# Finer setup loads and rewritten orders of all engines in a fused two-layer decoder kernel

## The chip, the cores and the metric

The kernel runs on one core of a Trainium2 chip. The metric is the device time of one execution in microseconds (us): the median of three runs. An engine is one of TensorE (PE in the profile, with its weight loads as PEld), VectorE (DVE), ScalarE (ACT), GpSimd (POOL) and SyncE (SP), which only issues DMA transfers here.

## What is computed

Input x has 32 sequences of 128 rows and 256 columns in float32. Six sublayers follow each other, each added to x and then normalised over its 256 columns:

```python
x = _layernorm(x + _L0_attn_ref(x, ...))                # 16 heads, a window of 7 keys, softmax times a learnt one
x = _layernorm(x + _L0_xattn_ref(x, ctx_1024, ...))     # cross attention, masked
x = _layernorm(x + _L0_ffn_ref(x, L0_ffn_Wr, ...))      # 8 experts pick 16 of 128 rows each, rope, attention, scatter back
x = _layernorm(x + _L1_attn_ref(x, ...))                # attention with a decay mask
x = _layernorm(x + _L1_xattn_ref(x, ctx_1024, ...))     # one context row chosen by argmax, then 16 heads
x = _layernorm(x + _L1_ffn_ref(x, ...))                 # quantised 256 -> 1024 -> 256 with a convolution and silu
```

The window attention is the part that the change touches most:

```python
scores = jnp.einsum('bhld,bhlwd->bhlw', Q, Kw) / np.float32(np.sqrt(DH))
fw = attn * conn
fw = fw / (fw.sum(axis=-1, keepdims=True) + 1e-09)
out = jnp.einsum('bhlw,bhlwd->bhld', fw, Vw)            # Kw, Vw: keys and values shifted by -3 to 3 rows
```

## The kernel before

The 32 sequences are worked on in 16 groups of two (256 rows). Each group passes nine stations, which the code names by a letter: Q (queries, keys and values of the window attention), A (the rest of the window attention), B (cross attention), X (experts), C (attention with decay), D (the choice of a context row), E (the 16 heads on it), F (the quantised feed-forward), and once, for the whole kernel, S (the setup: constants loaded, products of weights formed, the two feed-forward weights rounded). On every engine a station is a generator that stops at each `yield`; one stretch between two `yield`s is a step. A string of letters for each engine, `ORDER` (lines 68 to 121), says which station takes its next step, and `walk` plays it:

```python
for name in order:
    if name not in live or next(live[name], done) is done:
        live[name] = stations[name](next(left[name]))
        next(live[name])
```

So the tables fix the order of instructions on each engine, and semaphores alone fix the times: an engine that meets a wait stands there, and everything behind it in its table with it. Several groups are under way at once, each at another station. Banks of PSUM are tied to stations: Q and A share `bank_a`; B, C and D share `bank_c`; X has `bank_x`, F `bank_f`, E the four `banks_e`. Before a step writes a bank, `take` waits until the step that reads the last content is done, mostly a ScalarE copy (line 1377).

What the prediction speaks of, with its lines:
- SP's queue (lines 366 to 446) issues all transfers. In `setup`, S steps load weights: `wqkv_e` (3 MB) and `wo_e` (1 MB), the experts' weights, stand in the fourth loop over names (line 401). In `queries`, the second step waits for `a_v`, the copied values, and issues the twelve shifts (line 426): transfers inside SBUF that lay the values of a group one to three rows higher or lower. The next group's input `xT0` is loaded right behind (line 377).
- TensorE: Q's three steps project queries, keys and values (`wq0`, `wk0`, `wv0`, all by line 456). A's steps form head sums (line 562), turn the scores (line 570), turn the summed values (line 579, after `a_summed`) and project them with `wo0`. The next group's `wv0` has to wait for that projection's sum (`a_added`). B's first two steps are `w_cross` and `wv0x`.
- VectorE: A's window sum is thirteen steps (lines 1101 and 1105, `SUM_STEPS`), behind waits for all twelve shifts (`shift_in`) and the softmax weights. The same engine adds each sublayer's result to x (line 918) and forms, in the setup, the decay mask (lines 993 to 1006) and the column sums of the second feed-forward weight (line 1039).
- ScalarE rounds the two feed-forward weights in pieces (lines 1433, 1442, 1446); `small` is the sum of magnitudes that their scale needs, and `bank_f <- small` is the TensorE step that adds it over rows.

## Time and profile before

| | |
|---|---|
| median of 3 runs | 1081.63 us (1080.34 to 1083.15) |
| the profiled execution's own time | 1083.18 us |
| its span in the profile | 1081.4 us |
| instructions | 20184 |
| TensorE busy | 938.1 us, 87% |
| VectorE busy | 864.5 us, 80% |
| ScalarE busy | 774.6 us, 72% |
| GpSimd busy | 165.1 us, 15% |
| mean granted TensorE clock | 0.957 of 2.4 GHz |

All rows are of one profiled execution. Times count from the start of its span; the execution takes 1.8 us more than the span. A row in order of time reads: start, duration, engine, line, operation, what is written and what is read, count of merged instructions, and in brackets how long the engine was idle before and what released it.

### The profile page before, as it was taken

To read this page: it belongs to the slowest core of one execution; us is meant where nothing else is said; L and a number is where in the kernel's file an instruction comes from. 1 tells how busy PE (TensorE), PEld (TensorE's weight loads), DVE (VectorE), ACT (ScalarE), POOL (GpSimd) and SP (SyncE) were. 2 spreads that over 40 slices of the span, in tenths; PEclk is the share of its full clock that TensorE was granted. 3 is DMA by queue.
4 is the path that set the end of the run, shared out by engine and by line. 5 is a ranking of instruction groups with operands and counts; after the bars stand their busy time and mean duration, and the time that the engine had idled before them with its cause. 6 is when DMAs were issued, how large, how long until landed. Compare 5 with 4: busy or idle time off the path is not lost.

```text
span 1081.4 us, 20184 instructions
## 1 busy us (share of the span) xinstructions
PE 938.1 (87%) x7318; PEld 685.2 (63%) x7318; DVE 864.5 (80%) x2281; ACT 774.6 (72%) x1921; POOL 165.1 (15%) x404
## 2 busy tenths in 40 slices
PE   6588798999998999999999999999999888887652
PEld 4455566767776676767676777777676666565321
DVE  5585775789888979898899989898989785866754
ACT  2166564768877878877788878787878787867653
POOL 2010210202103030302021211212020201010000
PEclk9789999999999999999999999999999999998765
DMA  9723112030120203030302011121102000000000
...
DMA packets 36626, 59.04 MB, mean 55 GB/s; under 512 B 6656, under 2 KB 15872, under 8 KB 36016
## 3 DMA queue, kind: packets, MB, share of 16 engines
...
## 4 chain that ended last, share of the span: by engine, by line
PE 55%; ACT 18%; DVE 17%; issue 3%; SPq 2%; DMA 2%; POOL 1%; ACTq 0%; POOLq 0%; DVEq 0%
PE bank_c L456 15%; PE bank_a L456 8%; PE banks_e L456 6%; PE bank_x L456 6%; PE bank_f L456 4%; PE bank_x L666 3%; ACT squares_out L1389 2%; SPq L426 2%; ACT area_e L1605 2%; DVE area_f L1314 2%; DVE neg_top L1254 2%; PE banks_e L835 2%; DMA area_a<-in_xT 2%; ACT area_f L1652 2%; PE bank_a L562 2%
## 5 line engine op out<-in xcount | busy, mean ns | idle before, releaser
L1314 DVE SCALAR_TENSOR_TENSOR area_f<-area_f,w_convw 128x254 f32<-128x254 f32 x256 | 111.7, 478 | 9.2 <-ACT area_f L1639 7.5
L1254 DVE TENSOR_REDUCE neg_top<-banks_e 128x8 f32<-128x1024 f32 x64 | 76.2, 1220 | 30.1 <-PE banks_e L456 29.9
L1377 ACT ACTIVATE area_bx<-bank_x 128x512 f32<-128x512 f32 (+1 forms) x144 | 70.1, 499 | 27.7 <-PE bank_x L666 11.5
L1101 DVE TENSOR_TENSOR area_a<-area_a 128x512 f32<-128x512 f32 x112 | 74.7, 683 | 10.9 <-DMA area_a<-area_a 10.3
L1639 ACT ACTIVATE area_f<-area_f,w_convb,w_convw 128x256 f32<-128x256 f32 x128 | 69.8, 596 | 15.0 <-DVE area_f L1305 14.8
L1046 DVE TENSOR_TENSOR area_a<-area_a 128x512 f32<-128x512 f32 x112 | 73.4, 683 | 5.1 <-PE bank_a L562 2.9
L1605 ACT ACTIVATE area_e<-banks_e 128x512 f32<-128x512 f32 x128 | 68.3, 601 | 8.9 <-PE banks_e L835 8.7
L1377 ACT ACTIVATE area_bx<-bank_c 128x512 f32<-128x512 f32 x64 | 34.3, 536 | 52.9 <-PE bank_c L456 39.4
L1105 DVE TENSOR_TENSOR area_a<-area_a 128x512 f32<-128x512 f32 x96 | 65.8, 685 | 0.3
L1377 ACT ACTIVATE area_a<-bank_a 128x512 f32<-128x512 f32 (+1 forms) x80 | 43.9, 549 | 30.8 <-PE bank_a L456 21.2
L456 PE MATMUL bank_x<-area_bx 128*128 128x128 f32 (+1 forms) x256 | 51.9, 336 | 5.8 <-ACT area_bx L1377 4.3
L456 PE MATMUL bank_a<-area_a,w_wq 128*128 128x256 f32 x128 | 37.1, 442 | 19.1 <-DMA area_a<-in_xT 19.1
L456 PEld LDWEIGHTS bank_x<-area_bx 128*128 128x128 f32 x256 | 40.8, 191 | 17.5 <-ACT area_bx L1377 8.5
L1305 DVE TENSOR_TENSOR area_f<-bank_f,area_f 128x512 f32<-128x512 f32 x64 | 43.8, 684 | 7.7 <-PE bank_f L456 7.7
L456 PE MATMUL bank_f<-area_f,w1q 128*128 128x256 bf16 x256 | 41.8, 290 | 9.3 <-DVE area_f L1305 7.9
L1644 ACT ACTIVATE area_f<-area_f 128x512 f32<-128x512 f32 x64 | 40.4, 632 | 13.0 <-DVE area_f L1314 12.6
L1678 POOL TENSOR_SCALAR bn_negmean_b<-bn_sums_b 128x2 f32<-128x2 f32 x16 | 4.7, 294 | 288.8 <-DVE x L918 288.8
L666 PE MATMUL bank_x<-w_wqkv_e,area_bx 128*32 128x384 f32 x512 | 47.9, 492 | 0.0
L1377 ACT ACTIVATE area_e<-banks_e 128x256 bf16<-128x256 f32 (+1 forms) x64 | 34.5, 540 | 15.6 <-PE banks_e L821 6.8
L1324 DVE SCALAR_TENSOR_TENSOR area_f<-area_f 128x512 f32<-128x512 f32 x64 | 43.8, 684 | 2.1 <-ACT area_f L1644 1.5
L456 PE MATMUL banks_e<-chosen_key,chosen_q 32*128 32x256 f32 x512 | 38.6, 417 | 7.0 <-DVE neg_top L1254 3.9
L1652 ACT ACTIVATE area_f<-area_f 128x512 f16<-128x512 f32 x64 | 37.6, 624 | 9.4 <-DVE area_f L1362 9.4
...
## 6 DMA issues: line engine op xcount, KB each, us to landing
...
```

The costliest lines, as they stand in the source:

```text
L456: last = pe.matmul(out_ap, l, r, start=i == 0 and not opened, stop=closes and i == len(pairs) - 1)
L666: last = pe.matmul(bank_x[ES * q:ES * (q + 1), 0:3 * HP], xgf[:, c, e, :], wq[:, c, e, :], start=c == 0, stop=c == DC - 1)
L1046: return dve.tensor_tensor(product_of(wi).rearrange("p (n t) -> p n t", t=P), qT0.rearrange("p c (b t) -> p (c b) t", t=P), kT0.rearrange( ...
L1101: made[wi] = own.mark(dve.tensor_tensor(v4, v4, bc(e4[:, :, wi, :], 3, DH), ALU.mult))
L1105: added = dve.tensor_tensor(vw[:, to, :], vw[:, to, :], vw[:, wi, :], ALU.add)
L1254: dve.tensor_reduce(top[:, b, r:r + 2, :, 0].rearrange("p r (par c) -> p r c par", c=DC), banks_e[:, r:r + 2, :].rearrange("p r (c par k) ...
L1305: dve.tensor_tensor(blocks(th_f[jj % 3], 2), blocks(bank_f[:, :], 2), bc(tscale_f, 1, 2), ALU.mult).then_inc(f_h, 1)
L1314: last = dve.scalar_tensor_tensor(c4[:, i, :, dst], h4[:, i, :, src], cwt3[:, 2 * jj + i, k:k + 1], c4[:, i, :, dst], ALU.mult, ALU.add)
L1377: return act.activation(dst, src, ACT.Copy)
L1605: act.activation(pT_e[:, r * 4 * P:(r + 1) * 4 * P], bank_e[r][:, :], ACT.Exp, scale=float(DH) ** -0.5).then_inc(e_exp, 1)
L1639: last = act.activation(c4[:, i], h4[:, i], ACT.Identity, bias=w["convb"][:, j:j + 1], scale=cwt3[:, j, 1:2])
L1652: act.activation(n2_f[jj], c_f[jj], ACT.Copy, bias=ROUND16).then_inc(f_round, 1)
```

## The change

The setup's loads on SP are cut into smaller steps: 14 in place of 9. The six arrays of the connectivity network are a step apart from the other early constants, each of `wq0`, `wk0`, `wv0` is a step, and `wqkv_e` and `wo_e` are a step each. The first projection waits for `wq0` and the first input only; the wait for `wk0` and `wv0` stands ahead of the second. The tables of all five engines are new. No compute instruction is changed, added or left out. The diff, of whose tables one line each is shown:

```diff
 ORDER = {
     "PE": (
-        "QQQASSAASSSQBQBAADQSABBAASBBQBQXXBAAXSQXXABXBAAXBXQBXXBXXQXABAXCXQAXBXBXBABXACQXCXQCXXXCAXCAXBXQAXDDXDX"
+        "QQQASSSSSABABSQQDSAAQABABABBBSQXQXBAXAXQXABXABAXXBBXXQXBXQXBAXAXCQCXAXBAXABXBBQXCQXCXXCXCXAXAXBQDXADDXAX"
...
     "SP": (
-        "SQSBSASSSQQSSADSBQQQQBAAQQBADQQDBAQQBBQDQFAQQDFADBQQFBAFQQADBDQQFBAFAQBQDFBQAQDBQQFADFQDQABDFBAQDDFDFFFF"
+        "SSSQSSSSBASSSSQQSSDSABAAAAQQBQQBQQQDQBQQDBDQBQFAFDAQQBDFQAQBFDAQQBDFAQQBDFAQQBDFABQQDFABQQQFDAQBDFAQBDFD"
...
@@
             def setup(_):
-                for name in ("wq0", "wk0", "wv0"):
-                    sp.dma_start(w[name][:, :], io[name]).then_inc(qkv_in, 16)
-                yield
+                for name, sem in (("wq0", xt_in), ("wk0", kv_in), ("wv0", kv_in)):
+                    sp.dma_start(w[name][:, :], io[name]).then_inc(sem, 16)
+                    yield
                 for dst, name in ((c1, "c1"), (b1, "b1"), (c2, "c2"), (b2, "b2"), (c3, "c3"), (b3, "b3")):
                     sp.dma_start(dst, io[name]).then_inc(early2_in, 16)
+                yield
                 for name in ("pos", "ident", "headsum", "rows", "part", "wo0"):
                     sp.dma_start(w[name][:, :], io[name]).then_inc(early_in, 16)
                 yield
@@
-                for name in ("cos_sin", "blk", "iota128", "wqkv_e", "wo_e"):
+                for name in ("cos_sin", "blk", "iota128"):
                     sp.dma_start(w[name][:, :], io[name]).then_inc(xw_in, 16)
                 yield
+                for name in ("wqkv_e", "wo_e"):
+                    sp.dma_start(w[name][:, :], io[name]).then_inc(xw_in, 16)
+                    yield
@@
             def queries(g):
-                pe.wait_ge(xt_in, 16 * (g + 1))
+                pe.wait_ge(xt_in, 16 * (g + 2))
                 if g:
                     pe.wait_ge(a_heads, 2 * g)
-                if g == 0:
-                    pe.wait_ge(qkv_in, 16 * 3)
                 take("a")
                 project(bank_a, chunked("wq0"), xT0).then_inc(a_qk_proj, 1)
                 until("a", a_qk, 2 * g + 1)
                 yield
+                if g == 0:
+                    pe.wait_ge(kv_in, 16 * 2)
                 take("a")
```

Where the new tables put things is told by the instructions in their order, here at three places. **SP's queue around the first group's shifts**, before:

```order
L401 DMA w_iota<-in_iota 128x128
L401 DMA w_wqkv_e<-in_wqkv_e 128x6144
L401 DMA w_wo_e<-in_wo_e 128x2048
L426 DMA area_a<-area_a 112x512
L426 DMA area_a<-area_a 13x512
```

and now:

```order
L402 DMA w_iota<-in_iota 128x128
L405 DMA w_wqkv_e<-in_wqkv_e 128x6144
L405 DMA w_wo_e<-in_wo_e 128x2048
L430 DMA area_a<-area_a 112x512
L430 DMA area_a<-area_a 13x512
```

The experts' weights stand ahead of the first group's shifts (the 112-row and 13-row pieces of `area_a`) in both.

**TensorE from the last product of weights to group 0's window values**, before (`bank_e` holds products of weights; the `wq`, `wk` rows are group 1's, `w_cross`, `wv0x`, `headsum` group 0's):

```order
L456 MATMUL banks_e<-area_s,onesb 32x256
L456 MATMUL bank_a<-area_a,w_wq 128x256 [waits a_shifted,a_heads,xt_in]
L456 MATMUL bank_a<-area_a,w_wq 128x256 x3
L456 MATMUL bank_c<-area_bx,w_cross 128x256 [waits ctx_b_in,cross_in,setup_dve,setup_act]
L456 MATMUL bank_c<-area_bx,w_cross 128x256 x3
L456 MATMUL bank_a<-area_a,w_wk 128x256 [waits a_qk]
L456 MATMUL bank_a<-area_a,w_wk 128x256 x3
L466 MATMUL bank_c<-bias_parts,ones_bf 128x512 [waits b_kav]
L456 MATMUL bank_c<-w_wv0x,area_bx 128x256 x4
L579 MATMUL bank_a<-w_ident,area_a 128x128 [waits a_qk,a_summed]
```

and now:

```order
L460 MATMUL banks_e<-area_s,onesb 32x256
L566 MATMUL bank_a<-area_a,w_headsum 32x256 [waits a_prod]
L566 MATMUL bank_a<-area_a,w_headsum 32x256 x5
L460 MATMUL bank_c<-area_bx,w_cross 128x256 [waits ctx_b_in,cross_in,setup_dve,setup_act]
L460 MATMUL bank_c<-area_bx,w_cross 128x256 x3
L574 MATMUL bank_a<-w_ident,area_a 128x112 [waits a_scores]
L574 MATMUL bank_a<-w_ident,area_a 128x112
L470 MATMUL bank_c<-bias_parts,ones_bf 128x512 [waits b_kav]
L460 MATMUL bank_c<-w_wv0x,area_bx 128x256 x4
...
L460 MATMUL bank_a<-area_a,w_wq 128x256 [waits a_shifted,a_heads,xt_in]
...
L460 MATMUL bank_f<-small,onesb 128x1 [waits setup_act]
L583 MATMUL bank_a<-w_ident,area_a 128x128 [waits a_qk,a_summed]
```

Group 0's two projections of cross attention (`w_cross`, `wv0x`) stood behind group 1's first projection, which waits for `xt_in`; now they stand ahead of it. The line numbers are four higher in the changed kernel. The step on `small`, which waits for ScalarE's pass over the first feed-forward weight, now stands ahead of the turned values (`a_summed`).

**VectorE at group 2's window sum**, before (L1101 and L1105 are the sum's steps, `x_spread` belongs to group 0's experts):

```order
L1105 TENSOR_TENSOR area_a<-area_a 128x512 [waits dve_own]
L1204 RECIPROCAL area_bx<-area_bx 128x2 [waits x_exp]
L1101 TENSOR_TENSOR area_a<-area_a 128x512
L1105 TENSOR_TENSOR area_a<-area_a 128x512 [waits dve_own]
L1039 TENSOR_REDUCE area_s<-w2q 128x256 [waits setup_act]
L1101 TENSOR_TENSOR area_a<-area_a 128x512
L1105 TENSOR_TENSOR area_a<-area_a 128x512 [waits dve_own] x2
L1046 TENSOR_TENSOR area_a<-area_a 128x512 [waits a_qk]
L1046 TENSOR_TENSOR area_a<-area_a 128x512
L918 SCALAR_TENSOR_TENSOR x,bn_sums_x<-bank_x,x 128x256 [waits x_spread]
```

and now, first at two of group 2's key products and then at the end of the sum (line numbers are four higher):

```order
L1050 TENSOR_TENSOR area_a<-area_a 128x512
L1043 TENSOR_REDUCE area_s<-w2q 128x256 [waits setup_act]
L1050 TENSOR_TENSOR area_a<-area_a 128x512 [waits a_heads]
L1050 TENSOR_TENSOR area_a<-area_a 128x512
...
L1105 TENSOR_TENSOR area_a<-area_a 128x512
L1109 TENSOR_TENSOR area_a<-area_a 128x512 [waits dve_own]
L1105 TENSOR_TENSOR area_a<-area_a 128x512
L1109 TENSOR_TENSOR area_a<-area_a 128x512 [waits dve_own]
L1105 TENSOR_TENSOR area_a<-area_a 128x512
L1109 TENSOR_TENSOR area_a<-area_a 128x512 [waits dve_own] x2
L922 SCALAR_TENSOR_TENSOR x,bn_sums_x<-bank_x,x 128x256 [waits x_spread]
```

The reduction of `w2q` stood among the thirteen steps of the sum. It now stands between key products of the same group, behind a wait for ScalarE's finished rounding, and the sum ends without it.

## Rows read from the trace of the kernel before

**Rows 1.** The page's parts 1 and 2: busy time, the span in 40 slices.
```profile
PE 938.1 (87%) x7318; PEld 685.2 (63%) x7318; DVE 864.5 (80%) x2281; ACT 774.6 (72%) x1921; POOL 165.1 (15%) x404
...
PE   6588798999998999999999999999999888887652
```

**Rows 2.** Stretches: length; busy PE, PEld, DVE, ACT, POOL; clock, DMA share, GB/s.
```profile
60.00:120.00 60.00, 45.52 (x280) 32.61 (x273) 47.28 (x115) 37.16 (x83) 6.91 (x12) 0.90 0.25 74
...
200.00:840.00 640.00, 610.29 (x5006) 452.76 (x5004) 570.06 (x1516) 514.39 (x1301) 110.98 (x261) 1.00 0.17 50
...
960.00:1080.00 120.00, 67.10 (x458) 42.36 (x456) 75.37 (x172) 69.74 (x150) 8.33 (x24) 0.75 0.02 8
```

**Rows 3.** Issues on SP's queue, 16 to 28 us.
```profile
16.82 0.43 SPq L401 DMA_DIRECT2D w_wqkv_e<-in_wqkv_e  x1
...
18.50 8.73 SPq L426 DMA_DIRECT2D area_a<-area_a  x12
27.28 0.53 SPq L377 DMA_DIRECT2D area_a<-in_xT  x1
```

**Rows 4.** VectorE in order of time, 39 to 80 us.
```profile
39.72 1.89 DVE L1101 TENSOR_TENSOR area_a<-area_a 128x512 f32<-128x512 f32 x3 [10.32 <-DMA area_a<-area_a]
...
71.55 1.90 DVE L1101 TENSOR_TENSOR area_a<-area_a 128x512 f32<-128x512 f32 x3
...
78.19 1.41 DVE L1105 TENSOR_TENSOR area_a<-area_a 128x512 f32<-128x512 f32 x2
```

**Rows 5.** TensorE in order of time, 40 to 58 us.
```profile
40.19 3.78 PE L456 MATMUL bank_a<-area_a,w_wq 128*128 128x256 f32 x8 [9.62 <-DMA area_a<-in_xT]
43.76 3.13 PE L456 MATMUL bank_c<-area_bx,w_cross 128*128 128x256 f32 x8
48.56 1.99 PE L456 MATMUL bank_a<-area_a,w_wk 128*128 128x256 f32 x8 [1.67 <-ACT area_a L1377]
...
50.61 1.89 PE L456 MATMUL bank_c<-w_wv0x,area_bx 128*128 128x256 f32 x8
52.34 0.60 PE L579 MATMUL bank_a<-w_ident,area_a 128*128 128x128 f32 x4
...
56.78 1.97 PE L456 MATMUL bank_a<-w_wv,area_a 128*128 128x256 f32 x8
```

**Rows 6.** VectorE in order of time, 105 to 119 us.
```profile
105.75 0.48 DVE L918 SCALAR_TENSOR_TENSOR x<-bank_c,area_bx,x 128x256 f32<-128x256 f32 x1 [3.63 <-PE bank_c L456]
...
106.60 1.89 DVE L1101 TENSOR_TENSOR area_a<-area_a 128x512 f32<-128x512 f32 x3
...
112.69 3.64 DVE L1039 TENSOR_REDUCE area_s<-w2q 128x256 f32<-128x2048 f16 x1
...
116.85 1.40 DVE L1105 TENSOR_TENSOR area_a<-area_a 128x512 f32<-128x512 f32 x2
```

**Rows 7.** TensorE in order of time, 101 to 122 us.
```profile
101.33 3.44 PE L456 MATMUL bank_a<-area_a,w_wq 128*128 128x256 f32 x8 [1.99 <-DMA area_a<-in_xT]
104.61 1.03 PE L456 MATMUL bank_c<-area_bx 128*128 128x256 f32 x4
...
112.75 1.89 PE L456 MATMUL bank_x<-area_bx 128*128 128x256 f32 x8
118.31 1.12 PE L579 MATMUL bank_a<-w_ident,area_a 128*128 128x128 f32 x4 [3.67 <-DVE area_a L1105]
...
119.64 2.74 PE L456 MATMUL bank_c<-w_wv0x,area_bx 128*128 128x256 f32 x8
```

**Rows 8.** ScalarE in order of time: two pieces of the second weight's rounding.
```profile
82.90 1.91 ACT L1433 ACTIVATE w2q<-area_f 128x2048 f16<-128x2048 f32 x1
...
101.63 0.71 ACT L1446 ACTIVATE w2q<-area_f,small 128x512 f16<-128x512 f32 x1
```

**Rows 9.** TensorE's longest waits between 200 and 840 us: total, times, longest.
```profile
PE bank_c L456 <- ACT area_d L1377: 6.5, 14, 0.7
PE banks_e L456 <- ACT area_e L1377: 2.4, 5, 0.7
```

More of the change, by code:

```diff
@@ L97 @@
-        "FCFFFFEEFFFFFFFEEFFFDFDDFFFEFEEFFFEEEEEEFFFFFFFFEEFFFFFFFFFFFEEFFFFFFFEFFFFFFFFFFFFFFFFFFFFFFFFFFFFFFF"
+        "SSSSQQQQASSSSASASSSSSSSSSSSSSSSSSSSSSSSSSAASAAAAASSSSSSSSSSSAAAAAAAAAAAAASSSQQQQAASSSSSSAASSSBBAABAAAAAB"
+        "AAAAAAASAAAAAASXXXXXXXXXQXQQAAXQSAASXXXBBAAXXAAAAABBXAAAAAAAAAAAAAXQQQQAXXXAXXXXXXXXAAAABBAAXBAXXBAAAAAA"
+        "AAAXXACCXAAAAACQQQQCXAAXXXXXXAXXXADXXDDAAAAAAAAAAAAXXXAAAEEBBEXEEEEEBAXQBAAQXQQAAEECCCXEECEAAXXXXXXFFFXX"
+        "XDDDAAXXFEEFEFFEFEEEEFFBBFBFXXXFBFAFAFXFXAFAAFFAAFAAFCCEAEACXAAAAACAAAAFFFXFEEFQQQFFQEDDDXXXXXXAFFFFAXXX"
@@ new lines @@
+        "AXEEXAEEEEFEEFFFFBBFFBFFFFBXXXFFAAFFFEEAXAXAFXAAFACFCAAAFFCFAAAACEFEAFFFXQQQAAAEAQFXXXXXXXXFFFXAAXXDDDFA"
+        "EEFFEEFEEFEEFBBFFBXAFXBXFFFFAXAXFFAAAFEEXFFAAFAACCAACAAAAAACFFFAAEAXFEFQFFQQQEFAAXDDDFFFXXXXXXXXAEEXXAEE"
+        "FEEEEFFFFBBFFBFFFBFXFXFXAAFFFEFXEXFAAAXAAFAAACACAAAAAEECFFFXFFCFFAAQQQEFAAQFFFDXDDXXXXXAAXXFXFEFEFFEXEXF"
+        "FEEAEEFBBAFFXBXXFFBFFAAFFFXEXEAAAFXAAFAACCAAAAAFFFCAAEEFFFFCAXAAAFQQEQQXXXXXXXXDDDXAAFFFXXEEFEEFFFFEEFEB"
+        "EBFABAFFXXFBFXFFFAAFFFEAAXXFEAAAFCCAACAAAAAAAXAFFFCAXEEAAFFFFQQQQEFDDDFAXXXFFXXXAXXXEEXXFEEFFFEEFEAFEFBB"
@@ new lines @@
+        "FAFFBFXBXFFXFAAFFAAXXFFAAAXAAFCCFFAACEEFAAAAACXAFFEEAFFQQQQAAEDDDXXXXXFXFFFXXXAAEEXXEFEFFFFEEEBBFEFBFFAA"
+        "FFXXBXFFFFFAAEFFEAXXFAACAXFFCFAACAAAAACAEAAAEAAAXFFFFQQQEDDDQFXXXFFFXXXEEAAEEXEEFXEXEXFFFBFBFFBFXAAFFFXX"
+        "FXBFAFAFXEXEFFXAAAAAAAFAAFAAAACCFFCFAQAACEAEXAFQQFFFQEAAXXXXXXXXXFFFFXXAADDDFFEEFFEEFEEBEFBEFFBXXFFFFXBF"
+        "AAFFFFAFEXEXAFAAAXAACCAACAAAECAAAAFFXAEFAFFQQQQFFEXDXDDXXXFXXXAAFFFXEXEXFEEFEFFEEEFBFBFFBAFAFFXXFXFBFAFA"
+        "EFAEAAAAAAFFXXFCCXFFFAACAAEFEFCFFXAAAAAEAAFXDXXDDXXFAFFXXXXEEXXFEEFFFEEEEFBFBFFBFXXXFBFFFXXEEFFXFFFFCCFF"
@@ new lines @@
+        "XCXXACXCAXBXQDXADAXDAXBXDDDQBXBCBQEXEEEEXBECXBXCEEEEXECCXECADXCEXDXAEDAQFFDFDDDXFBBFFBXAFFEBXBFFEEEEXFCA"
+        "EFFCBQFXCFXBXCQCXEEEEXCEDCXDFFEXDXAFFEXEADFQDDDAFFFBFBXFBXFEFFBEEFFBEEFXFECAFXABCFQFXCEFBXEEXECQECXXCDFF"
+        "FEXFCXXEXBADEFDFFFAQDFXDDDFABBFXFFXEBFBFFEEEEXAFCEFABCFXFBFXCEEEEXCECXQXCQDCXDEAFFDFFXEXFEXAFQDFDDDFAFBB"
+        "XFBEXFFFBEEFBFEEAFXECFFBCFXFBAXCFXEEXEEQXECXQCXEFCFFFXCDEDXFEDFXAFFDFADDDFAQBFFFBXBFXEFBXEEBEEAFFFCXEAFB"
+        "CXFBFCXQXEEEDEXCEXCFFQFFCXECXXDEXFDAFEDADDDFFAQFBFBXBFFXFBFEXBFFEEEECAFEFFCAXFQBXCFXBXCQXEEEECXECXDCEFDF"
@@ new lines @@
+        "AFFXDEXEFDXADDDFFFQAFBFBXFBFFXFEBFBXFEEFEEAFCEXFABCFXBQCFXXCXDXCEEEECEXCQDFEXDFFFXEXEDAFDDDFAFFBFAFBFBQX"
+        "FFBXFFBEFXFEEEEACFFECFAXBCFXBXEEEECXQECXCXQCDDEXFDFFFXXEDAXEDDDFFFFBAFBAFQBXFFFBXBFFEXFEEEEFAFEXCFABXCQX"
+        "FBCFXQXEEEECXCECDXEACXXFFEFFXBEQDAFDAFFFXDFADDDFXBFFBXFBEFFCFBEEEEFXFAEFBFCFBXCEEEXECXECXQXCDCXDQEXXDFFF"
+        "XFEAEDFDDDFFFAFQBAFBXBFFFBXFFEFXEEBEEAFFECFABFXCBEECFXEXEXCEXCXFFECFFDCXDEXXDAXEFDFDDDFFAFBAFBXBFFFXBEFF"
+        "XBFEEEEXBECFFXCXFFBCXFEEEEXCEXFCFFFXECDXXCEDXFEDFFFFDDDDXFXCFCFFXCFFFECFCEEEFXFECFEFCDXDEEXEEFDXFEXFFXEX"
@@ L112 @@
+        "DEXDDDEFCFCFFCFEFCEFCFEEEFCDFEFFCEFFEEEDFFEFDEFFDFFDDDEFEFFFFEFEEEEFFFEFFFEFFFEEEFFEEFFFFEFEFFFFFFFFFFFF"
         "FFFFFFFFFF"
@@ L114 @@
     "POOL": (
[L115 removed]
+        "ABABXABCXABXCEABCXEAFBCXEFABCXEFABXCEFABCXFEABCXEFABCXEFABCXEFABCXEAFBCXEFABCXEFABXCEFCXEFCEFEFF"
     ),
     "SP": (
[L118 to L119 removed]
+        "SSSQSSSSBASSSSQQSSDSABAAAAQQBQQBQQQDQBQQDBDQBQFAFDAQQBDFQAQBFDAQQBDFAQQBDFAQQBDFABQQDFABQQQFDAQBDFAQBDFD"
+        "FDFFFF"
     ),
```

51 lines of the change are left out of this document (12 added, 39 removed).

## The prediction

> **What bounds the kernel now.** The page's busy shares come first: TensorE is busy 87% of the span, VectorE 80% [rows 1]. The 40 slices say where the rest is: TensorE's digits are 5 to 8 in the first five slices, 8 or 9 in nearly all of the middle, and fall over the last six [rows 1]. So there are three regimes, and the table of stretches gives their size [rows 2]. Between 200 and 840 us TensorE works 610.3 of 640 us: 29.7 us, 5%, are left. In the last 120 us it works 67.1, and the granted clock is 0.75 there: the last groups go through F alone, each step waiting for the one before. Between 60 and 120 us it works 45.5 of 60 us: too few groups are under way.
>
> The order of time shows what holds the beginning. SP issues the experts' weights at 16.8 us and the first group's shifts from 18.50 to 27.23 us [rows 3]. VectorE starts the window sum at 39.72 us after 10.3 us of idleness that a transfer ends [rows 4], and TensorE starts group 1's query projection at 40.19 us after 9.6 us, ended by the input that was issued at 27.28 us [rows 3, 5]. From there the window attention is a chain over groups: values of group g copied, twelve shifts issued (8.7 us), window sum, values turned and projected with `wo0`, sum added to x, values of group g+1 projected. What shortens this chain early starts everything else earlier, as every transfer that sets a fixed time lies before 50 us.
>
> **The wait at 39.7 us stays.** The finer setup steps would allow the experts' 4 MB to be issued after the shifts. The instructions in order say that they are not: `wqkv_e` and `wo_e` stand directly ahead of the shifts as before. The shifts then queue behind the same bytes, and I cost the loads' part at nothing. The two waits on `wk0`/`wv0` and on `xT0` gain nothing either: the input is issued last of the four, and the first projection waits for it. The table's new place of the first x and context loads is covered by the same wait.
>
> **Start, group 0 and 1: -3.2 us.** TensorE now does group 0's `w_cross` and `wv0x` in the idle stretch before 40 us; before, they lay between group 1's query projection and group 0's value turning (3.13 and 1.89 us at 43.76 and 50.61 [rows 5]). VectorE's decay products, which lay among the thirteen sum steps, move there too. So after 39.72 the sum takes 8.05 us (thirteen steps undisturbed: from 71.55 to 79.60 [rows 4]) and ends at 47.8. TensorE: query projection 40.19 to 44.0 (3.78), a copy of some 0.6, key projection 2 to 3 us, another copy: 48.3. The step on `small` waits for the first feed-forward weight, which ScalarE reads by about 47.5. I let the value turning start at 48.9. From it to the next value projection it is 4.44 us now (52.34 to 56.78 [rows 5]): 53.4 against 56.78, so 3.4 less, of which I take 3.2. The cover that has to hold is VectorE's: softmax of group 0 and the decay mask must end before 39.7. By the durations of the same instructions they end at about 39.2; if not, up to 1 us is lost.
>
> The clock: the query projection at 40.19 took 3.78 us and the key projection at 48.56 took 1.99 for the same eight matmuls [rows 5]; TensorE had been idle 9.6 us before the first. I assume 3.78 again, since an idle stretch of only 1.99 us also had 3.44 behind it at 101.33 [rows 7]. The Trainium skill (TensorE: Matmul & The Clock Gate, What's actually happening) says that activity releases the throttle; by it the two projections moved into the gap could keep the array at 2.4 GHz and give 1.8 us more. That is not in the sum.
>
> **Group 2: -4.8 us more.** Before, VectorE's sum of group 2 was held twice. First by its place behind group 1's cross attention result, idle 3.63 us to 105.75 [rows 6]: TensorE had group 3's query projection ahead of that product, which waited for its input and ran 3.44 us [rows 7]. In the new table the product stands ahead of the query projection. Second by the reduction of `w2q` among the steps, 3.64 us at 112.69 [rows 6]; now it is done earlier, in front of two key products, where VectorE has gaps. With the 3.2 us from before, the sum could end 10.5 us earlier than its 118.25, at 107.8. TensorE waited 3.67 us for it at 118.31 [rows 7]. Now TensorE is the later one: from 101.33 to the end of the experts' product at 112.75 + 1.89 = 114.64 it had 13.3 us, less 1.4 for what went ahead and 1.5 at full clock, plus 2 for `wv0x` of group 2, now in front of the turning (2.74 at the lower clock, at 119.64 [rows 7]). Starting with the input at 98.1, the turning comes at about 110.5 instead of 118.3. I take 8.0 us for the beginning in all. Bounds: 3.2 if nothing of group 2 comes, 10.5 if all of it does.
>
> **Middle: -4.5 us.** The macro order is the same: 97% of TensorE's 952 steps stand within five places of where they stood. So what is won at the beginning moves the middle as a whole; it isn't lost in it. What changes is how often two steps of one station follow each other directly, so that the second waits for the copy of the first: on TensorE 75 pairs before and 42 now, in the middle (142nd to 810th step) 25 and 5. What such a pair costs is in the waits: 14 of D's cost 6.5 us, 5 of E's 2.4 us [rows 9], about 0.47 us each. Twenty pairs fewer are 9.4 us of the 29.7 at most. The waits are ended by ScalarE and VectorE, and VectorE works 570 of the 640 us [rows 2]: TensorE, coming earlier, will meet some of them at the next step. I take half, 4.5 us (bounds 0 and 9.4; below 0 is the slower rival's case). The Trainium skill (Trace Analysis, Matmuls) wants independent groups to rotate through PSUM banks so that a copy overlaps the next group's matmuls; here pairs on one bank fall from 78 to 46, and by that rule all 9.4 would come.
>
> **End: -1.0 us.** In the last 142 steps pairs fall from 28 to 22, worth at most 2.8 us, but the last 19 steps are the same and wait for each other. I take 1.
>
> **SP's queue** is passed in another order too: the store of group 1 and the load of x for group 7 now stand ahead of group 7's shifts. Group 1's result was ready 9 us before those shifts were issued, so this costs nothing; x of groups 2 to 5 is loaded at once near 40 us, 1 MB that nobody waits for.
>
> **The sum.** 8.0 + 4.5 + 1.0 = 13.5 us. The profiled execution took 1083.2 us, which makes 1069.7; the median of the runs is 1.6 us lower, so the forecast is **1068 us**.
>
> **Rivals.**
> - *Only the start comes* (0.20): TensorE is so full after 125 us, and its waits so much those of other engines, that the middle gives nothing and group 2 little: 3.2 us, 1078.4 us. For it: 5% idle in the middle is close to full. Against it: the 3.67 us at 118.31 are plainly TensorE's and go.
> - *All waits go* (0.10), as the rule on banks has it: 10.5 + 9.4 + 2.8 = 22.7 us, 1059 us. Against it: VectorE at 89% in the middle.
> - *The rounding becomes the bound, slower* (0.08): VectorE's reduction of `w2q` waits for ScalarE's last piece. Before, ScalarE began the second weight at 82.90 and ended at 102.34 [rows 8], without anybody waiting. Now group 2's key products, head sums and softmax are queued behind it on VectorE. If ScalarE ends only at 99 (3.2 earlier), the reduction ends at 102.7, the sum starts 8 us later, at about 110.5 instead of 106.6, and the kernel takes 4 us more: 1085.6 us. The new table puts all eight pieces ahead of the experts' gathered rows, so by it they should be done at about 83. It decides from 95 us on. Other slower orders, a bank held in the middle, get 0.01.
> - *The change does more than the order tells* (0.01): if the shifts landed before the experts' weights, the sum would start 10 us earlier: 1058 us.
>
> The forecast itself has 0.60. About 0.3% (3.2 us) is what a measurement can tell from no change: 1078.4 to 1084.8 is "same". Half of the first rival lies there, the rest of it is faster. Faster 0.80, same 0.11, slower 0.09. The range from 1059 to 1079 us holds the forecast with all its bounds, the first rival and about half of the second.
>
> **What would show it.** In the changed profile the first sum step starts at 39.7 us still; group 1's value projection at about 53.5; group 2's value turning at 110 to 111; the reduction of `w2q` lies between 84 and 90 us; the stretch from 200 to 840 has 612 to 616 us of TensorE work; waits of `bank_c` for `area_d` fall from 14 to about 4; the last 120 us look the same. I am wrong if the value turning of group 2 comes after 115, or if the middle's idle time is 30 us or more.

## The result, and the profile after

| | before | changed |
|---|---|---|
| median | 1082.39 us (1080.34 to 1085.33, 4 runs) | **1053.27 us** (1051.58 to 1054.91, 4 runs) |
| ratio | | 0.973, 95% interval 0.970 to 0.976 |
| profiled execution / its span | 1083.18 / 1081.4 us | 1052.96 / 1051.2 us |

It is 29 us faster, where 13.5 were forecast, and lies 6 us below the range of 1059 to 1079 us. The page of the changed kernel, parts 1 and 2, against [rows 1]:

```profile
PE 932.7 (89%) x7318; PEld 681.6 (65%) x7318; DVE 868.3 (83%) x2281; ACT 774.7 (74%) x1921; POOL 159.9 (15%) x404
...
PE   6779989999999999999999999999899999876642
```

The work is the same 7318 matmul records, and they take 5.4 us less of busy time, in part because fewer of them run at the lower clock (below, at group 2); the fifth slice (105 to 131 us) went from 7 to 9, and there are three digits of 8 where there were nine. Once one kernel is ahead, the same moment finds the two at different work. But 97% of TensorE's steps stand within five places of where they stood, so the number of matmul records that are done is a ruler that both share ("equal progress" from here on). First the kernel before, cut at 120, 240 and 840 us, then the changed one, cut where it had done as many (columns as in [rows 2]):

```profile
0.00:120.00 120.00, 83.35 (x450) 60.57 (x451) 80.09 (x202) 50.17 (x111) 14.40 (x36) 0.89 0.51 166
120.00:240.00 120.00, 109.98 (x849) 80.74 (x851) 81.97 (x228) 73.33 (x195) 16.66 (x44) 0.99 0.20 62
240.00:840.00 600.00, 573.42 (x4721) 424.97 (x4713) 540.83 (x1434) 486.31 (x1229) 105.52 (x245) 1.00 0.16 49
840.00:1082.00 242.00, 171.33 (x1311) 118.88 (x1307) 161.62 (x419) 164.78 (x388) 28.53 (x79) 0.86 0.04 11
```

```profile
0.00:107.00 107.00, 81.85 (x450) 59.26 (x451) 81.18 (x203) 50.58 (x111) 15.02 (x37) 0.90 0.58 191
107.00:222.20 115.20, 108.80 (x844) 79.46 (x846) 82.57 (x225) 73.31 (x191) 16.87 (x44) 1.00 0.19 60
222.20:815.30 593.10, 573.27 (x4729) 425.08 (x4722) 542.69 (x1435) 486.10 (x1231) 100.77 (x244) 1.00 0.16 49
815.30:1052.00 236.70, 168.81 (x1307) 117.80 (x1305) 161.85 (x421) 164.69 (x391) 27.30 (x80) 0.87 0.03 11
```

So 13.0 us are won by the old 120 us, 4.8 from there to 240, 6.9 in the middle (TensorE's idle time there: 26.6 us before, 19.8 now) and 5.5 at the end (counted to the ends of the spans, 1081.4 and 1051.2). The forecast had 8.0 for the first two together, 4.5 and 1.0.

**The start.** SP's queue, VectorE and TensorE of the changed kernel in order of time, against [rows 3 to 5]:

```profile
18.06 8.73 SPq L430 DMA_DIRECT2D area_a<-area_a  x12
```

```profile
38.66 1.90 DVE L1105 TENSOR_TENSOR area_a<-area_a 128x512 f32<-128x512 f32 x3 [0.68 <-DMA area_a<-area_a]
```

```profile
32.06 1.89 PE L460 MATMUL bank_c<-w_wv0x,area_bx 128*128 128x256 f32 x8
...
39.13 3.78 PE L460 MATMUL bank_a<-area_a,w_wq 128*128 128x256 f32 x8 [0.49 <-DMA area_a<-in_xT]
43.59 3.78 PE L460 MATMUL bank_a<-area_a,w_wk 128*128 128x256 f32 x8 [0.69 <-ACT area_a L1381]
...
48.42 0.64 PE L583 MATMUL bank_a<-w_ident,area_a 128*128 128x128 f32 x4
...
52.90 1.96 PE L460 MATMUL bank_a<-w_wv,area_a 128*128 128x256 f32 x8 [0.96 <-DVE x L922]
```

The transfer still ends the wait ahead of the sum. That it comes 1.06 us earlier is no more than scatter: in the profiles below with SP's old order the sum starts at 39.1 to 40.7 us, in those with the new one at 38.6 to 40.0 (run 13, the same kernel again: 39.99). Of VectorE's 10.32 us of idleness there 0.68 are left, as setup work fills them. Group 1's value projection comes at 52.90 (forecast 53.5, before 56.78).

**Group 2**, against [rows 6, 7]:

```profile
84.26 3.81 DVE L1043 TENSOR_REDUCE area_s<-w2q 128x256 f32<-128x2048 f16 x1
...
97.58 1.87 DVE L1105 TENSOR_TENSOR area_a<-area_a 128x512 f32<-128x512 f32 x3
...
104.19 1.41 DVE L1109 TENSOR_TENSOR area_a<-area_a 128x512 f32<-128x512 f32 x2
```

```profile
97.22 1.99 PE L460 MATMUL bank_a<-area_a,w_wq 128*128 128x256 f32 x8
...
107.81 0.60 PE L583 MATMUL bank_a<-w_ident,area_a 128*128 128x128 f32 x4
...
112.80 1.89 PE L460 MATMUL bank_a<-w_wv,area_a 128*128 128x256 f32 x8
```

The values are turned at 107.81 instead of 118.31, and nothing is waited for there; group 3's value projection follows at 112.80, where before it came at 126.02: 13.2 us earlier. TensorE, before, between the rows of [rows 7]:

```profile
105.47 0.38 PE L492 MATMUL bank_x<-w_ident,area_bx 128*128 128x128 f32 x2
106.33 0.71 PE L456 MATMUL bank_x<-area_bx 128*128 128x128 f32 x4 [0.47 <-ACT area_bx L1377]
...
109.92 1.07 PE L456 MATMUL bank_x<-w_wo_e,area_bx 128*32 128x256 f32 x16 [0.69 <-ACT area_bx L1377]
```

The clock is part of it. Before, it was granted at 0.66 on average from 100 to 105 and from 117 to 122 us (query projection 3.44 us, `wv0x` 2.74 [rows 7]); in the changed kernel it is whole there, and the two take 1.99 and 1.89 us:

```profile
72.00:952.00 880.00, 833.80 (x6792) 615.70 (x6790) 758.93 (x2016) 694.23 (x1756) 143.26 (x356) 1.00 0.15 45
```

**The middle.** TensorE's longest waits, 200 to 840 us, against [rows 9]:

```profile
PE bank_c L460 <- ACT area_d L1381: 2.7, 6, 0.8
PE banks_e L460 <- ACT area_e L1609: 2.2, 6, 0.6
```

The two kinds of waits that I had priced (for the copies into `area_d` and `area_e`) had 6.5 + 2.4 us; the first has 2.7 now, in 6 waits, and the second is no longer in the list. The row of `area_e` shown is another wait of E, for ScalarE's exponentials (line 1609); before it had 0.6 us.

### The profile page after: what moved, and what is told of

It reads as the page before. It is cut to its first block, busy times and chain, and to the rows that moved or that the text cites. A ratio compares the mean times of both kernels' runs of the same rounds, so it can differ in the third digit from the quotient of the medians.

```text
span 1051.2 us, 20184 instructions
## 1 busy us (share of the span) xinstructions
PE 932.7 (89%) x7318; PEld 681.6 (65%) x7318; DVE 868.3 (83%) x2281; ACT 774.7 (74%) x1921; POOL 159.9 (15%) x404
## 4 chain that ended last, share of the span: by engine, by line
PE 58%; ACT 18%; DVE 16%; issue 3%; SPq 2%; POOL 2%; DMA 1%; ACTq 0%; POOLq 0%; DVEq 0%
PE bank_c L460 16%; PE bank_a L460 8%; PE banks_e L460 6%; PE bank_x L460 6%; PE bank_f L460 4%; DVE neg_top L1258 3%; DVE area_f L1318 3%; ACT area_e L1609 3%; PE bank_x L670 3%; ACT squares_out L1393 2%; PE banks_e L839 2%; PE bank_a L566 2%; ACT area_f L1643 2%; ACT area_f L1656 2%; DVE x L922 2%
## 5 line engine op out<-in xcount | busy, mean ns | idle before, releaser
L1258 DVE TENSOR_REDUCE neg_top<-banks_e 128x8 f32<-128x1024 f32 x64 | 76.0, 1221 | 17.9 <-PE banks_e L460 17.5
L1381 ACT ACTIVATE area_bx<-bank_x 128x512 f32<-128x512 f32 (+1 forms) x144 | 70.4, 500 | 25.2 <-PE bank_x L670 11.5
L1105 DVE TENSOR_TENSOR area_a<-area_a 128x512 f32<-128x512 f32 x112 | 74.7, 683 | 1.3 <-DMA area_a<-area_a 0.7
L1309 DVE TENSOR_TENSOR area_f<-bank_f,area_f 128x512 f32<-128x512 f32 x64 | 43.7, 683 | 12.7 <-PE bank_f L460 12.5
L1648 ACT ACTIVATE area_f<-area_f 128x512 f32<-128x512 f32 x64 | 40.7, 636 | 13.0 <-DVE area_f L1318 12.8
L460 PE MATMUL banks_e<-area_e,chosen_v 128*32 128x512 f32 x256 | 35.0, 620 | 11.9 <-ACT area_e L1609 11.6
L1366 DVE TENSOR_TENSOR area_f<-area_f,bank_f 128x512 f32<-128x512 f32 x64 | 40.5, 679 | 3.1 <-PE bank_f L862 3.1
## 6 DMA issues: line engine op xcount, KB each, us to landing
w_wqkv_e<-in_wqkv_e SPq DMA_DIRECT2D x1, 3072.0 KB, 12.6
area_f<-in_raw SPq DMA_DIRECT2D x2, 1024.0 KB, 10.5
```

Source lines behind the costliest of these rows:

```text
L460: last = pe.matmul(out_ap, l, r, start=i == 0 and not opened, stop=closes and i == len(pairs) - 1)
L1105: made[wi] = own.mark(dve.tensor_tensor(v4, v4, bc(e4[:, :, wi, :], 3, DH), ALU.mult))
L1258: dve.tensor_reduce(top[:, b, r:r + 2, :, 0].rearrange("p r (par c) -> p r c par", c=DC), banks_e[:, r:r + 2, :].rearrange("p r (c par k) ...
L1381: return act.activation(dst, src, ACT.Copy)
```

## Experiments

All kernels but the repeat of the changed one are the changed code with other tables. A station's steps are written with their group and number, `D6.4` is the fifth step of D for group 6. Several tables are spliced by time: of one kernel's table the steps that it had taken by a time T, and behind them all others in the other kernel's order:

```diff
-table = new
+table = new[:n] + (old, without the steps that stand in new[:n])
 n: steps taken by T  53 us: PE 20, DVE 82, ACT 20, POOL 1, SP 26     115 us: PE 66, DVE 181, ACT 86, POOL 6, SP 29
                     240 us: PE 189, DVE 373, ACT 226, POOL 16, SP 38  840 us: PE 805, DVE 1419, ACT 1029, POOL 81, SP 98
```

**1. The old orders in the new code** (table of all engines = old, SP's setup letters written out).

> The changed kernel with the tables of before (SP's nine setup letters written out as fourteen, so that the transfers stand in the old order); only the finer steps and the two waits of the first projection are left of the change. Both theories (each head start of a beginning is kept to the end; each gives part of it back) expect no change here: 1079 to 1085 us, ratio 0.997 to 1.003. If the loads' part alone made more than 3 us, my term of nothing for it would be wrong.

Measured: 1084.03 us, ratio 0.9994 (0.9967 to 1.0021). The finer loads and the two waits are worth nothing by themselves.

**2. New orders up to 53 us, then old.**

> New tables up to the point that the changed kernel had reached at 53 us (group 1's value projection), from there the remaining steps in the order of before. By PE's progress the changed kernel is then 3.7 us ahead. Theory 'kept' (what is won early stays): 1079 us (1077 to 1080.5). Theory 'only the start comes' of the prediction would have the same number. Rival 'the start is the root of the whole early gain' (the 13 us at 120 us follow from it): 1065 to 1072 us. Rival 'given back' (the old order behind it waits for its transfers anyway): 1082 us.

Measured: 1080.55 us, ratio 0.9969 (0.9944 to 0.9994): 3.4 us, with an interval from 0.6 to 6.1 us.

**3. New orders up to 115 us, then old.**

> New tables up to the changed kernel's 115 us (just behind group 3's value projection), then the order of before. PE's progress is 13 us ahead there. 'Kept': 1069 us (1067 to 1072). 'Given back' (group 3 and 4 of the old order wait elsewhere, for ctxT_d and the experts): 1074 to 1080 us.

Measured: 1070.80 us, ratio 0.9890 (0.9864 to 0.9915): 11.9 us.

**4. New orders up to 240 us, then old.**

> New tables up to the changed kernel's 240 us, then the order of before. PE's progress is 17.5 us ahead there. 'Kept': 1065 us (1062 to 1068); my forecast's 8 us for the beginning would give 1074 us. 'Given back': above 1070 us. If it comes near 1053 us, the middle and the end of the new tables are worth nothing by themselves.

Measured: 1070.32 us, ratio 0.9873 (0.9837 to 0.991): 13.8 us, between the two. What became of the rest the table below shows.

**5. The mirror: old up to 240 us, then new** (n of the old tables: PE 169, DVE 339, ACT 197, POOL 15, SP 39).

> The mirror of the last one: orders of before up to its 240 us, then the changed kernel's. If the gains of beginning and rest add up, this one has what the new beginning lacks: 29 us less some 14, so 1069 us (1066 to 1072). By the forecast's terms (4.5 for the middle, 1 for the end) 1078 us. If the new middle is only good behind its own beginning: above 1074 us.

Measured: 1071.37 us, ratio 0.9872 (0.9845 to 0.9899). 13.6 us: two halves that add up to the 29.

**6. New up to 840 us, then old.**

> New orders up to the changed kernel's 840 us, then the order of before: what the new end is worth. By PE's progress 5 us: 1058 us (1056.5 to 1060). By the forecast's term of 1 us: 1054 us. If the end of the old order loses more behind a new middle: above 1060 us.

Measured: 1056.46 us, ratio 0.9731 (0.9705 to 0.9757). Run 8, which has the new end and differs from the changed kernel in SP's table alone, took 1053.70 beside it: the new end is worth some 3 us (the runs lie from 1054.8 to 1058.4 and from 1052.8 to 1054.3), less than the 5.5 us between the two profiles. The ratios to before, 0.973 here and for the changed kernel, are too coarse to show it.

**7. The middle's pairs broken in the old order** (27 swaps in TensorE's table, such as):

```diff
-A9.wo F5.0 D6.4 D6.5 Q10.wv E6.0
+A9.wo F5.0 D6.4 Q10.wv D6.5 E6.0
```

> Orders of before, but in TensorE's middle (142nd to 810th step) each pair of steps on one bank is broken by moving the step behind it in between: 25 pairs become 1, all else is as before. The prediction's term says 24 pairs of 0.47 us, half to all of it: 1072.5 to 1079 us. Rival 'pairs are worth nothing by themselves' (the waits are ended by ScalarE and VectorE, which are late on their own account): 1083 to 1085 us. Above 1086: the step moved ahead waits longer than the pair did.

Measured: 1111.86 us, ratio 1.024 (1.020 to 1.028): **27 us slower**. TensorE's waits, 200 to 840 us:

```profile
PE bank_f L903 <- ACT area_f L1656: 5.8, 2, 3.5
PE banks_e L460 <- ACT chosen_v L1381: 5.1, 6, 2.0
PE bank_a L583 <- DVE area_a L1109: 4.3, 3, 2.5
PE bank_c L491 <- ACT x L1400: 3.1, 3, 2.5
...
PE bank_c L460 <- ACT area_d L1381: 1.1, 4, 0.4
```

The waits of the pairs went as priced, from 14 and 6.5 us to 4 and 1.1. In their place stand waits of up to 3.5 us of steps that had at most 1.0 us in all before. `chosen_v` is what D's last step hands to its group's E, and nine of the swaps delay a D's last step by one place; how each of the other waits follows from a swap is not shown. Waits are not all of it either: at equal progress (cut as above) the middle is 22 us longer, of which 8 are busy time, at a clock of 0.99 on average instead of 1.00:

```profile
243.50:865.30 621.80, 581.56 (x4721) 430.46 (x4713) 541.17 (x1434) 486.38 (x1230) 104.94 (x245) 0.99 0.15 47
```

**11. Only 14 of these swaps**, in those places where the new table has the two steps the same way round (25 pairs become 12).

> Orders of before, but only those 14 swaps of neighbouring TensorE steps of the middle that break a pair on one bank and in which the changed table has the two in the swapped order as well (25 pairs become 12). By the price in the prediction, 13 x 0.47 = 6 us at most, half of it 3: 1078 to 1082 us. Rival 'a swap alone gives nothing, since the moved step waits in its turn': 1083 to 1087 us; the run with 27 swaps lost 27 us, by its scale 14 swaps would lose up to 14: 1098 us.

Measured: 1086.56 us, ratio 1.0029 (0.9998 to 1.0061): nothing won. The same view:

```profile
PE banks_e L460 <- ACT chosen_v L1381: 3.9, 4, 2.0
PE bank_c L460 <- ACT area_d L1381: 3.2, 8, 0.7
PE bank_c L496 <- DVE area_d L1244: 2.2, 2, 1.8
```

Half of the pairs' waits went (6.5 to 3.2), and `chosen_v` took over as much.

**17. Twenty pairs made again in the new order** (5 pairs on one bank become 28):

```diff
-A5.wo F0.8 D2.4 Q6.wv D2.5 F1.0 A6.hs1
+A5.wo F0.8 D2.4 D2.5 Q6.wv F1.0 A6.hs1
```

> The changed kernel, with 20 of the pairs that before had in TensorE's middle made again, each by moving one step by one or two places; 5 pairs on one bank become 28. 'The pairs are what the new middle took away': 23 x 0.4 to 0.47 = 9 to 11 us, 1063 to 1065 us, as with the whole old middle (1064.8), and the waits of bank_c and banks_e for the copies come back. 'A pair's wait is only taken over from the next one': 1054 to 1058 us. Both can hold in part, since in the runs with pairs broken the moved steps waited in their turn.

Measured: 1077.65 us, ratio 0.9942 (0.9924 to 0.9959): some 24 us of the 29 gone. TensorE's waits, 222 to 840 us:

```profile
PE bank_c L460 <- ACT area_d L1381: 7.1, 11, 1.3
PE bank_x L460 <- ACT area_bx L1381: 3.3, 5, 1.8
PE banks_e L460 <- ACT area_e L1381: 2.8, 2, 2.1
```

```profile
229.00:842.40 613.40, 576.49 (x4723) 425.36 (x4712) 541.66 (x1430) 486.68 (x1230) 100.11 (x244) 1.00 0.16 48
```

The pairs' waits are back, and dearer than priced. The next table takes TensorE's idle stretches of over 0.2 us in the middle, at equal progress, and splits them by whether the instruction ahead of the gap wrote the same bank, which is what a pair does (us, worked out from the traces):

| run | length of the middle | TensorE busy | idle | behind the same bank | other waits |
|---|---|---|---|---|---|
| before | 600.0 | 573.4 | 26.6 | 12.5 | 11.0 |
| changed | 593.1 | 573.3 | 19.8 | 1.7 | 14.0 |
| 16, old middle (below) | 599.1 | 573.1 | 26.0 | 12.5 | 10.5 |
| 7, pairs broken | 621.8 | 581.6 | 40.2 | 0.5 | 36.3 |
| 11, 14 swaps | 604.5 | 576.3 | 28.2 | 6.4 | 18.7 |
| 17, pairs back | 613.4 | 576.5 | 36.9 | 17.9 | 15.0 |

Of the 20 us that run 17's middle is longer than the changed kernel's, 16 stand behind the same bank, 0.7 us for each of the 23 pairs, and 3 are busy time. Run 7 got rid of 12 us of pairs' waits and took on 25 us of others; the new order got rid of 11 and took on 3. So pairs cost, but breaking them pays only where the moved step isn't late for something else. By the medians it is about 1 us a step in runs 7 and 17 (27 for 27 swaps, 24 for 20), in run 11 a fifth of that, which is within its noise.

One rival stays untested. Runs 7, 11 and 17 change TensorE's table alone, while the changed kernel rewrites all five. For 12 of run 7's 27 swaps ScalarE still copies the two results in the old order (in the one shown, those of `D6.5` ahead of that of `Q10.wv`). What the same swaps cost with ScalarE's and VectorE's tables following, no run shows.

**8. The experts' weights really behind the first shifts and input** (SP's table of the changed kernel):

```diff
-"SSSQSSSSBASSSSQQSSD
+"SSSQSSSSBASSQQSSSSD
```

> The changed kernel, with the experts' two weights issued behind the first group's shifts and the next input instead of ahead of them (what the finer steps allow and the new table does not use). 'Transfers of 4 MB hold the sum': group 1's query projection comes near 31 us and the sum at about 35, 4 us earlier, and the kernel takes 1049 to 1051 us. 'Given back': the weights of the feed-forward and the experts come later, and the chain from 55 us on waits for other things: 1052 to 1055 us. Slower than 1056 us if the experts of group 0 wait for wqkv_e at about 85 us.

Measured: 1053.70 us, ratio 0.9705 (0.9683 to 0.9727), as the changed kernel. The sum now waits for nothing, but starts only at 38.12 us, as VectorE is busy with the decay mask until then:

```profile
38.12 1.90 DVE L1105 TENSOR_TENSOR area_a<-area_a 128x512 f32<-128x512 f32 x3
```

**12. The same, with the setup work that stood ahead of the sum put behind it** (tables of the changed kernel; `S35` to `S45` of VectorE are the decay products, `S5` and `S6` TensorE's two small products, `S8` ScalarE's pass over the first feed-forward weight):

```diff
-PE  S5 Q1.wq Q1.wk D0.0 S6 A0.val A0.wo Q1.wv
+PE  Q1.wq Q1.wk A0.val A0.wo S5 Q1.wv D0.0 S6
-DVE S35..S45 A0.10..A0.22 S46 S47 S48 Q1.0 Q1.1 Q1.2 Q1.3 A0.23 A1.0
+DVE A0.10..A0.22 S35..S45 Q1.0 A0.23 Q1.1 Q1.2 Q1.3 S46 S47 S48 A1.0
-ACT S7 Q1.0 S8 Q1.1 D0.0 A0.2 A0.3 Q1.2 A0.4
+ACT Q1.0 Q1.1 A0.2 S7 S8 A0.3 Q1.2 D0.0 A0.4
```

> The changed kernel with the experts' weights behind the first shifts and input, and the work that then stands ahead of the first window sum moved behind it: VectorE's decay products, TensorE's two small setup products and group 0's context keys, ScalarE's pass over the first feed-forward weight. The sum should start near 34.6 instead of 38.7 and group 1's value projection near 48 instead of 52.9. 'Kept': 4 to 5 us, 1048.5 to 1050 us. 'Given back' (rounding, ctxT_d and group 2's input come no earlier): 1052 to 1054 us.

Measured: 1054.90 us, ratio 0.9748 (0.9708 to 0.9787): given back. TensorE in order of time:

```profile
34.97 1.89 PE L460 MATMUL bank_a<-area_a,w_wq 128*128 128x256 f32 x8
37.55 1.99 PE L460 MATMUL bank_a<-area_a,w_wk 128*128 128x256 f32 x8 [0.69 <-ACT area_a L1381]
...
50.69 1.97 PE L460 MATMUL bank_a<-w_wv,area_a 128*128 128x256 f32 x8 [0.85 <-DVE x L922]
...
59.70 1.93 PE L566 MATMUL bank_a<-area_a,w_headsum 128*32 128x256 f32 x12 [3.60 <-DVE area_a L1050]
```

The input had landed by 34.97 us and the shifts by 35.96, when the sum starts, and the value projection came 2.2 us earlier; then the second head sum waits 3.60 us for VectorE's key products, which stand behind the moved setup work, and starts at 59.70 where the changed kernel had it at 58.24. In runs 8 and 12 VectorE's work, not the 4 MB, sets the time up to 60 us. No version that I tried beats the changed kernel.

**9. Two edits alone on the old orders**, those of my term for group 2:

```diff
-PE  B1.tr X0.7 Q3.wq B1.pv X0.8 X0.9
+PE  B1.tr X0.7 B1.pv Q3.wq X0.8 X0.9
-DVE A2.18 A2.19 S60 A2.20 A2.21 A2.22 Q3.0 Q3.1 X0.17 A2.23
+DVE A2.18 A2.19 A2.20 A2.21 A2.22 S60 Q3.0 Q3.1 X0.17 A2.23
```

(`S60` is the reduction of `w2q`, `A2.10` to `A2.22` the window sum, `X0.17` group 0's expert result added to x.)

> Orders of before with the two edits on which my term for group 2 rests, and nothing else: group 1's last product of cross attention ahead of group 3's query projection on TensorE, and the reduction of w2q behind group 2's window sum instead of in it. By the prediction's working: the sum ends 7.3 us earlier (near 111), TensorE is then the later one and turns the values near 115, 3 us earlier; 3 to 4.8 us in all, 1079 to 1081 us. Rival 'TensorE's late inputs, not VectorE, set it': less than 1 us, 1083 to 1085 us.

Measured: 1078.63 us, ratio 0.9972 (0.994 to 1.0005): 3 us by the ratio, whose interval reaches to no change, 5 by the medians. In its trace the value turning comes at 113.08, and:

```profile
119.69 0.66 PE L491 MATMUL bank_c<-w_ident,x 128*128 128x128 f32 x4 [1.66 <-ACT x L1400]
120.85 1.99 PE L460 MATMUL bank_a<-w_wv,area_a 128*128 128x256 f32 x8
```

Group 3's value projection comes 5.2 us earlier than 126.02 (1.1 us of lead were there at 100 us already, ahead of the edits), with a new wait ahead of it for the normalised x of the experts, whose sum now stands behind the reduction.

**10. Two TensorE moves more** (`X0.8 X0.9` ahead of `Q3.wq`, `B2.wv0x` ahead of `A2.val`, ScalarE's copies in the same order).

> As the last, and two more that the new table makes at this place: the turning and exponents' products of group 0's experts (two steps) ahead of group 3's query projection, and group 2's wv0x ahead of its value turning (ScalarE's copies follow suit). Theory 'I stopped counting at the value turning': what counts is group 3's value projection, before at 126.0; here it comes at 119 to 121 and the kernel takes 1076 to 1079 us. Rival 'these two only swap places': the same as the run with two edits, within 1 us.

Measured: 1080.71 us, ratio 0.9977 (0.9954 to 0.9999). From the last product of cross attention to the value projection it takes 21.3 us (101.56 to 122.86), with two edits 20.9 (99.96 to 120.85). The theory that these moves bring the rest of the gain fell: they only swap places.

**15. The reduction moved further back** (as 9, `S60` behind `Q3.3`, ahead of `X1.0`), beside **14. the reduction put back into the sum of the changed kernel** (`S60`, and its cast `S61`, ahead of `A2.20`) and **13. the changed kernel again**.

> As the run with two edits on the orders of before, but with the reduction of w2q behind group 0's expert result and group 2's attention result as well, where VectorE idles anyway. 'It held more than the sum': TensorE's wait of 1.66 us for the normalised x goes, the value projection of group 3 comes near 119 instead of 120.9, and the kernel is 1.5 to 2.5 us faster than with two edits (ratio to before 0.993 to 0.995). Otherwise as with two edits (ratio 0.995 to 0.997).

> The changed kernel with one VectorE step put back where before had it: the 3.8 us reduction of w2q among the last steps of group 2's window sum. Theory 'it held more than the sum' (behind it on VectorE stand the sum's end and group 0's expert result, for whose normalised rows TensorE's next product and group 3's value projection wait): the value projection comes 3 to 4 us later than 112.8 and the kernel takes 1056 to 1058 us. By the prediction's working, where TensorE is the later engine at this place: under 2 us, 1055 us at most.

> The changed kernel once more, beside the three that follow, so that differences of 2 to 4 us can be read on one chip: 1052 to 1055 us.

Measured: 13: 1054.03 us. 14: 1056.83 us, 2.8 us slower, though the runs overlap (1053.3 to 1057.4, and 1051.7 to 1055.7); group 3's value projection at 118.61 instead of 112.97, of which 1.2 us were behind before the reduction was reached. 15: 1082.96 us, ratio 0.999 (0.9966 to 1.0014): everything lost that two edits had brought. In 14 the clock has a share, as 3.38 us for `wo0` are not the 1.89 of run 13:

```profile
113.83 0.61 PE L470 MATMUL bank_a<-bias_parts,ones_bf 128*128 128x512 bf16 x1 [1.49 <-ACT area_a L1381]
114.23 3.38 PE L460 MATMUL bank_a<-w_wo,area_a 128*128 128x256 f32 x8
```

The trace of 15 shows where its loss is. Group 3's value projection comes at 120.24, even 0.6 us earlier than in run 9; behind it, VectorE and TensorE:

```profile
120.58 3.72 DVE L1043 TENSOR_REDUCE area_s<-w2q 128x256 f32<-128x2048 f16 x1
```

```profile
127.14 0.36 PE L650 MATMUL bank_x<-w_ident,area_bx 64*128 64x64 f32 x1 [3.14 <-DVE area_bx L1166]
```

The 3.7 us now hold the routing of group 1's experts. So behind 100 us it costs in the places that were tried: 4 us more here than right behind the sum (run 9), and 2.8 more inside the sum (run 14) than at 84 us. At 84 us it costs nothing that can be seen: run 14, without it there, is not ahead at 100 us.

**16. The old middle between new beginning and new end** (new up to 240 us, the old order of those steps that new takes up to 840 us, then new).

> New orders up to 240 us and from 840 us on, the order of before between: what the new middle is worth in the new kernel. By idle time at equal progress 6.8 us: 1060 us (1058 to 1061.5). By the prediction's term 4.5 us: 1057.5 us. If the old middle hands on 3 to 4 us more loss to the end, as behind a new beginning alone: 1062 us or more.

Measured: 1064.76 us, ratio 0.9819 (0.9788 to 0.985): 10.7 us slower than the changed kernel beside it. In the profiles 6 to 7 us of the 11 between them lie in the middle, 2 behind it, and 2 ahead of it, where the tables are the same, which is scatter.

The splices show how a gain lives on. How many us a kernel is ahead of the profile before when it has done as many matmul records (worked out from counts in stretches of 4 us, good to about 1 us; last column by the spans):

| run | 60 | 100 | 120 | 240 | 360 | 600 | 840 | 960 | end |
|---|---|---|---|---|---|---|---|---|---|
| changed | 3.7 | 5.7 | 13.1 | 17.8 | 21.6 | 24.0 | 24.7 | 29.3 | 30.2 |
| 2, new to 53 | 3.3 | 2.7 | 3.6 | 2.9 | 2.4 | 2.6 | 1.6 | 0.5 | 2.3 |
| 3, new to 115 | 5.2 | 6.0 | 12.6 | 13.9 | 12.7 | 13.1 | 12.3 | 12.4 | 15.1 |
| 4, new to 240 | 5.0 | 6.0 | 13.7 | 18.2 | 17.4 | 17.9 | 16.0 | 13.0 | 12.7 |
| 5, old to 240 | 1.3 | 0.0 | 1.6 | 0.4 | 4.2 | 6.8 | 8.0 | 12.4 | 13.8 |
| 14, reduction back | 2.5 | 4.0 | 10.7 | 11.5 | 15.9 | 18.0 | 18.8 | 24.2 | 25.8 |
| 16, old middle | 2.8 | 5.1 | 12.0 | 15.2 | 15.9 | 15.8 | 16.0 | 16.2 | 19.2 |
| 6, new to 840 | 2.8 | 4.9 | 12.6 | 16.8 | 21.0 | 23.6 | 24.4 | 24.4 | 27.2 |

Through the middle a lead is kept to some 2 us over 600 us (runs 2, 3, 4). The end is another thing: run 4 loses 3 us there, run 5 gains 6. One profile scatters by some us at the end (run 1, equal by its median, had a span of 1089.0), so only the medians carry a verdict there.

## Where the prediction was right, and where it failed

The direction held, and so did the claim that a lead of the beginning moves the middle as a whole; the splices show it. The size was less than half, and the time lies below the range. The step that failed is the term for the beginning: 8.0 us, bounded at 10.5. The traces have 17.8 us at the old 240 us, 9.8 of the 16.7 that are missing there. The chain of group 2 was cut off too early in it (13.0 us are won by the old 120 us), and the stretch from 120 to 240 us was put at nothing without a reason (4.8 us). By the splices the beginning is 13.7 us, 5.7 more than its term, and the middle, 10.7 by run 16, is as far off. Term by term:

- **Loads: 0.** Right (run 1). The 4 MB still stand ahead of the shifts, and the wait ends when it did, within the scatter.
- **Start: -3.2 us.** Right, 3.4 us in run 2, though that run's interval is nearly as wide as the term. The working holds too. In the first profile two departures cancel, the sum 1.06 us earlier and the key projection at 3.78 us where 2 to 3 were allowed; in run 13, the same kernel, the sum starts at 39.99, the key projection takes 1.99 us and the value projection comes at 53.14, where 53.4 was worked out. The cover held, VectorE was done 0.7 us before the transfer.
- **Group 2: -4.8 us.** Too small: runs 2 and 3 give 8.5 us (11.9 less 3.4; 9.8 by the medians), the traces 9.3. The two edits on which it rests measured 3 to 5 us alone, as priced. The rest is in the working. I closed the sum at the value turning, where 5.0 us follow until group 3's value projection that were 7.7 before, since `wv0x` had gone ahead: I charged its 2 us ahead of the turning and did not credit its leaving from behind. I let TensorE need 12.4 us from the query projection to the turning, and it needed 10.6: two pieces of work went ahead, the product of cross attention (0.86 us, 104.61 to 105.47) and the two steps of the experts (1.41 us, 105.47 to 106.88), and I took off 1.4 for one; the wait of 0.69 us ahead of `wo_e` went too. And I took the input of group 3 for the start, 98.1, where the query projection began at 97.22. That is 2.7 + 1.8 + 0.9 us, and with the 7.8 by which my turning was earlier (118.3 to 110.5, which the sum carries as 8.0) it makes the 13.2 of the trace. It is read off the traces: no single edit that brings it was found (run 10 added nothing). Runs 9, 14 and 15 show that the place of the 3.7 us reduction is part of it.
- **120 to 240 us: no term at all.** 4.8 us in the trace, 3.6 of them idle time of TensorE. With the old order behind it 3 to 4 us of this are kept up to 840 us (runs 3 and 4 in the table), and then the end takes it: the medians of the two differ by 0.5 us.
- **Middle: -4.5 us.** The mechanism was right and the size too small: 6.9 us in the two traces, 10.7 by run 16, of which only 6 to 7 are lost within the middle. I priced the waits of D and E alone, 8.9 us; with those of the other stations the pairs stood for 12.5 us, and 10.8 of them went. I let half of it be met again at the next step; it was 3.0 us. The price does not carry over to swaps by hand: breaking 24 pairs cost 27 us, making 23 cost 24. The rule of the Trainium skill (Perfetto Trace Analysis, Matmuls), by which groups that rotate through banks overlap their copies, is true of these waits (12.5 to 1.7 us in the changed kernel, to 0.5 in run 7); in run 7 it gives the wrong sign of the time, as the other waits grow by more.
- **End: -1.0 us.** Some 3 us by run 6, 5.5 in the traces, above the bound of 2.8. What won it stays open.
- **The rivals.** The rounding never decided: ScalarE's last piece ends at 82.4 us, and the reduction starts at 84.26 behind other work. "All waits go" was nearest, and still 6 us short, as it had the same closed term for group 2.
- **The signs of being wrong** (a turning behind 115 us, 30 us of idle time in the middle) looked at the slow side alone, and neither came. The value turning at 107.81 instead of 110 to 111 and 618.5 us of TensorE work from 200 to 840 us, where 612 to 616 were forecast, told of the other side.
